# Window attention with turned keys and turned queries copied out of PSUM by two engines

## The chip, the cores and the metric

The kernel runs on one core of a Trainium2 chip. The metric is the device time of one execution in microseconds (us), lower is better. A core has TensorE (PE in the rows: matmuls and transposes; PEld is its weight load), VectorE (DVE), ScalarE (ACT), GpSimd (POOL) and the sync engine SyncE (SP), which here only issues DMAs. Each engine takes its instructions in the order in which the program gives them; the engines are tied together by semaphores written out by hand.

## What is computed

A Swin-style block on a (4, 32, 32, 128) image, then a single-head self-attention over the 1024 tokens of each image. What matters here is the first attention:

```python
xn = _layer_norm(x, norm1_g, norm1_b)               # 64 windows of 64 tokens after a roll
qkv = xw @ qkv_w.T + qkv_b                           # 16 heads of 8 channels
q = _rope2d(q, tabs); k = _rope2d(k, tabs)
attn = einsum('bhnd,bhmd->bhnm', q * scale, k) + attn_mask
attn = softmax(attn, axis=-1)
out = einsum('bhnm,bhmd->bhnd', attn, v)             # then projection, residual
# then layer norm, a gated MLP (fc1, silu, fc2), and x + y
# second block: f = x Wq, g = x Wk, h = x Wv; gamma * softmax(f g^T) h + x
```

## The kernel before, in words

The 64 windows are taken two at a time: 32 pairs of 128 tokens. Values of fp32 are split into an fp16 high part and an fp16 low part, so that TensorE can work in fp16. A software pipeline of steps n = -2 to 34 runs over the pairs; the same `body(n, ...)` is written once for each engine, and the order of its parts is the order in which the engine works. Steps 12 to 27 are a hardware loop of 8 steps, the others are written out.

In step n TensorE (`pe_pairs`, lines 908 to 968) does: the projection of queries and keys of pair n+2 (L917), the turn (transpose) of queries and keys of pair n+1 into the bank `T1_BANK` (L932, L933; the helper's line is L904), the scores of pair n with the mask (L938; helper lines L876, L885), whose row maxima VectorE takes (L1075), the scores in the turned direction of pair n-1 (L949; L876, L897), probabilities times values of pair n-3 (L956), the value projection of pair n-1 (L964), and the turn of the queries with their maxima for pair n (L968). `t1_ps` is one PSUM bank of 2 KB per partition seen as fp16: half 0 holds the turned queries, half 1 the turned keys, 512 elements each.

In step n VectorE multiplies by the rotary tables for pair n+2 (L1048, `ta`, `tb`), copies both halves of `t1_ps` for pair n+1 to `qk_t` (L1060) and signals `qt_ready`, subtracts for `v_lo` (L1068), takes the maxima (L1075), splits them (L1080, L1082), and so on. SyncE waits for `qt_ready` and then issues four DMAs (L836) that put the turned keys from `qk_t` into `k_t`; they signal `kz_ready`, for which the scores of the next step wait (L936).

In step n ScalarE (L1149 to L1209) writes `q_rows` and `k_rows` (L1158, L1161; all copies have the helper's line L1117) from the rotated values `rot` that GpSimd has made (L1253), then in some steps `ln_hi_of` (below), the exponential (L1187, `e_buf`), the copy of the turned queries with maxima (`q_t`), two halves of `v_hi`, and `p_hi`.

The layer norm of the input goes in 8 chunks of 512 tokens. Chunks 2 to 7 are turned by TensorE in steps n = 1, 3, 5, 7, 9 and 11 (`LN_STEP`), in the bank `T1_BANK` too, between the scores of pair n and the turned scores of pair n-1:

```python
if ln_chunk(n):
    pe.wait_ge(qt_ready, n + 2)      # T1_BANK has been copied out for pair n+1
    ln_turn(ln_chunk(n))             # L845
```

ScalarE then copies the turned chunk (`xn_all`, `ln_hi_of`), VectorE subtracts (`ln_lo_of`, L1011). For chunks 4 to 7 ScalarE also normalises two tiles of `xn` at the end of each of the steps 3 to 10 (L1208). In steps 28 and later the MLP's first work is mixed in. The time after 205 us (MLP and second attention) is not touched.

Of the kernel before, what the change touches and what calls it, by code (L numbers as in the profile page):

```python
# [26 lines left out]
PAIRS = WPAIRS * B  # L27
# [25 lines left out]
def build(nc, t):  # L53
    ctx = ExitStack()
    with ctx:
# [3 lines left out]
        def sem(name):  # L59
            return ctx.enter_context(nc.semaphore(name))  # L60
# [120 lines left out]
        lo_done = sem("lo_done")  # L181
        t1_done = sem("t1_done")
        qt_ready = sem("qt_ready")
        kz_ready = [sem(f"kz_ready{u}") for u in range(2)]
        s_done = sem("s_done")
        max_done = sem("max_done")
# [12 lines left out]
        def wait(eng, s, value):  # L199

            if not isinstance(value, int) or value > 0:
                eng.wait_ge(s, value)
# [135 lines left out]
        def mlp_pe(pe):  # L338
# [37 lines left out]
            def turn_a_waits(c):  # L376
                pe.wait_ge(a_lo, c + 1)
                wait(pe, at_ready, c)
                if at_bank(c) == PRJ_BANK:
                    pe.wait_ge(x1_ready, c)  # L380
# [83 lines left out]
            def early(left):  # L464
                if left == 5:

                    pe.wait_ge(rope_done, PAIRS)
                    turn_a_waits(0)
                    turn_a(0, 0)
                if left == 4:  # L470

                    pe.wait_ge(qt_ready, PAIRS)
                    pe.wait_ge(proj_w_lo, 1)
                    project(0, 0)
                if left == 3:

                    bias()
                if left == 2:

                    pe.wait_ge(fc1_b_ready, 1)  # L480
                    turn_a_waits(1)
                    turn_a(1, 1)
                    pe.wait_ge(mlo_done, PAIRS)
                    turn_y(0, 0)
                if left == 1:

                    pe.wait_ge(exp_done, PAIRS)
                    pe.wait_ge(fc1_w_lo, 1)
                    fc1(0, 0, 0)

            def bias():

                pe.wait_ge(rest_loaded, REST_LOADS)
                pe.wait_ge(at_ready, 1)
                for k in range(2 * HBLK):
                    last = pe.matmul(ps[:, at_bank(0), k:k + 1], fc1_w[:, 128 * k:128 * k + 128], g1b1[:, 3:4],
                                     start=True, stop=True)
                last.then_inc(fc1_b_sum, 1)

            return body, early, bias  # L500

        def mlp_dve(dve):
# [240 lines left out]
        with ExitStack() as st:  # L743
# [15 lines left out]
            qk_t = tmp("qk_t", [128, 2, 2, 4, 128], F16)  # L759
# [11 lines left out]
            t1_ps = ps[:, T1_BANK, :].bitcast(F16).rearrange("p (a c q) -> p a c q", a=2, c=4)  # L771
# [34 lines left out]
            def at_step(n, step):  # L806
                return isinstance(n, int) and n == step

            def valid(n, lag):
                return not isinstance(n, int) or 0 <= n - lag < PAIRS  # L810
# [29 lines left out]
            def pe_pairs(pe):  # L840
# [38 lines left out]
                def scores(queries, keys, w, parts):  # L879

                    masked(S_BANK, w, 0, parts)
                    for c in range(4):
                        for e in range(2):
                            rows = slice(64 * e, 64 * e + 64)
                            last = pe.matmul(  # L885
                                ps[rows, S_BANK + c // 2, 256 * (c % 2):256 * (c % 2) + 256]
                                .rearrange("p (h k) -> p h k", h=4),
                                queries[:, c, rows], keys[:, :, c, rows], start=False, stop=True, skip_group_check=True)
                    return last
# [18 lines left out]
                def body(n, it, w, parts):  # L908
                    r = w % BUFS
                    u = r % 2  # L910
                    v = 1 - u

                    if valid(n, -2):
                        wait(pe, rope_done, n + 2)

                        pe.wait_ge(ln_ready, (n + 2) // TPC + 1 if isinstance(n, int) and n < LOOP_FROM else CHUNKS)
                        project(qkv_ps[:, 0:2 * DIM], n + 2, slice(0, 2 * DIM)).then_inc(qk_done, 1)  # L917
                    if at_step(n, -2):

                        pe.wait_ge(mask_top, 1)  # L920
                        pe.matmul(ps[0:1, T1_BANK, 0:1], mask_max[:], ln_const[:, 2, 0:1], start=True,
                                  stop=True).then_inc(mask_summed, 1)
                    if at_step(n, -1):

                        pe.wait_ge(mask_known, 1)
                        rest.append(pe.value_load(mask_any[0:1, 0:1].bitcast(mybir.dt.int32)))
                    if valid(n, -1):
                        wait(pe, lo_done, n + 2)
                        wait(pe, qt_ready, n + 1)
                        if ln_chunk(n, 1):  # L930
                            pe.wait_ge(ln_ready, ln_chunk(n, 1) + 1)
                        turn(t1_ps[:, 0], q_rows[:, (r + 1) % BUFS])  # L932
                        turn(t1_ps[:, 1], k_rows[:, v]).then_inc(t1_done, 1)  # L933
                    if valid(n, 0):

                        pe.wait_ge(kz_ready[u], it * 64 + 64)  # L936
                        wait(pe, mlo_done, n)
                        scores(qk_t[:, u, 0], k_t[:, r], w, parts).then_inc(s_done, 1)  # L938
                    if ln_chunk(n):

                        pe.wait_ge(qt_ready, n + 2)
                        ln_turn(ln_chunk(n))
                    if valid(n, 1):

                        wait(pe, q2_ready, n)
                        wait(pe, exp_done, n - 1)
                        if at_step(n, 1):
                            pe.wait_ge(ln_ready, 2)
                        scores_turned(k_t[:, (r - 1) % BUFS], q_t2[:, v], (w - 1) % WPAIRS, parts).then_inc(st_done, 1)  # L949
                    if valid(n, 3):  # L950
                        wait(pe, plo_done, n - 2)
                        wait(pe, norm_done, n - 3)
                        for hp in range(HP):
                            out = pv_ps[:, hp].rearrange("p e r d -> p (e r d)")
                            for k, (p, vals) in enumerate(((p_hi, v_hi), (p_hi, v_lo), (p_lo, v_hi))):
                                last = pe.matmul(out, p[:, v, 2 * hp:2 * hp + 2, :].rearrange("p h q -> p (h q)"),  # L956
                                                 vals[:, v, hp].rearrange("p e r d -> p (e r d)"),
                                                 start=(k == 0 and hp == 0), stop=(k == 2), skip_group_check=True)
                        last.then_inc(pv_done, 1)
                    if valid(n, 1):  # L960

                        wait(pe, vlo_done, n - 1)
                        wait(pe, q2_ready, n)
                        project(v_ps, n - 1, slice(2 * DIM, 3 * DIM)).then_inc(v_done, 1)  # L964
                    if valid(n, 0):
                        wait(pe, mlo_done, n + 1)
                        wait(pe, q2_ready, n)
                        turn(t2_ps, q_rows[:, r]).then_inc(t2_done, 1)  # L968
                    if at_step(n, -2):
                        ln_turn(1)  # L970
# [11 lines left out]
            def _(dve):  # L982
# [55 lines left out]
                def body(n, it, w):  # L1038
                    r = w % BUFS
                    u = r % 2  # L1040
                    v = 1 - u
# [15 lines left out]
                    if valid(n, -1):  # L1057

                        dve.wait_ge(t1_done, n + 2)
                        dve.tensor_copy(qk_t[:, v], t1_ps).then_inc(qt_ready, 1)  # L1060
                    if at_step(n, -1):
                        ln_stats_of(3)
                    if valid(n, 2):
# [42 lines left out]
            def _(act):  # L1106
# [9 lines left out]
                def copy(out, in_):  # L1116
                    return act.activation(out, in_, ACT.Copy)  # L1117
# [31 lines left out]
                def body(n, it, w):  # L1149
                    r = w % BUFS  # L1150
                    u = r % 2
                    v = 1 - u
                    if isinstance(n, int):
                        mlp_act(act)[2](LAST - n)
                    if valid(n, -2):

                        act.wait_ge(r_done, n + 3)
                        copy(q_rows[:, (r + 2) % BUFS, :, 0:16].rearrange("p h (r d) -> p h r d", r=2),  # L1158
                             rot[:, u, 0].unsqueeze(2).broadcast_to([128, HEADS, 2, HD]))
                        wait(act, t1_done, n + 1)  # L1160
                        copy(k_rows[:, u].rearrange("p h (r d) -> p h r d", d=HD)[:, :, 0:3:2, :],  # L1161
                             rot[:, u, 1].unsqueeze(2).broadcast_to([128, HEADS, 2, HD])).then_inc(hi_done, 1)
                    if at_step(n, -2):
                        ln_hi_of(1)
                    if at_step(n, -1):
# [682 lines left out]
```

## Time and profile before

| | us |
|---|---|
| median of 3 runs | 410.07 |
| lowest, highest run | 408.0, 411.35 |
| the profiled execution's time | 408.14 |
| its span (first to last instruction) | 406.3 |
| steps 3 to 12 (window of 38 to 88 us): TensorE busy | 45.70 of 50.00 |
| same window: ScalarE, VectorE busy | 43.34, 42.23 |
| steps 13 to 29 (88 to 175 us): TensorE busy | 83.98 of 87.00 |
| same window: ScalarE, VectorE busy | 68.74, 74.96 |

The profile is of one execution; 1.8 us of its time lie outside the span. Busy times count an instruction from its start to its end, also where it overlaps the next one on its engine, so a share near 90% can be an engine without a gap. The chain of waits follows the last instruction back to what released it.

### The profile page before, as it was taken

Reading aid. Unit: us, or ns where it says so; the run is one execution under the profiler, and the core shown is the slowest. Engines: PE = TensorE matmul, PEld = TensorE weight load, DVE = VectorE, ACT = ScalarE, POOL = GpSimd, SP = SyncE. Lnnn points to the kernel's source line nnn. Section 1 sums busy time; section 2 is a strip of 40 time slices with the busy share of each in tenths; the row PEclk is TensorE's granted clock in tenths of the full one; section 3 lists DMA queues with packets and bytes.
Section 4 is the critical chain, followed back from the end, with each engine's and each line's share of the span. In section 5 each row is a group of like instructions: output and inputs, shape, how many; then the busy total and the mean of one; then the engine's idle time right before and its main releaser. Section 6 shows DMA issues by size and latency. Waiting matters only on the chain.

```text
span 406.3 us, 12124 instructions
## 1 busy us (share of the span) xinstructions
PE 357.3 (88%) x4700; PEld 223.4 (55%) x4700; DVE 300.9 (74%) x830; ACT 272.5 (67%) x436; POOL 261.0 (64%) x314
## 2 busy tenths in 40 slices
PE   2487999899998999998599999999989989989692
PEld 0244665555565666667355345553546757667472
DVE  6668888888888888887746767778657797884524
ACT  3467988887777787887635554444767867768480
POOL 7467967666767777797658665564235865868330
PEclk9999999999999999999989999999999999999787
DMA  5701110001101011110000100000101011010101
GB/s 173 250 15 27 29 27 26 25 24 30 31 27 29 25 29 29 29 29 3 0 3 2 26 2 0 2 2 0 28 0 28 2 52 27 2 54 2 53 2 55
DMA packets 15594, 12.19 MB, mean 30 GB/s; under 512 B 3991, under 2 KB 14136, under 8 KB 15544
## 3 DMA queue, kind: packets, MB, share of 16 engines
q1 hardware_dynamic: 14208, 10.96, 9.4%
q8 instruction: 34, 0.56, 0.6%
q10 hardware_dynamic: 1336, 0.54, 0.5%
q14 instruction: 16, 0.13, 0.1%
HBM read 4.15 MB, written 2.10 MB: 15 GB/s over the span
## 4 chain that ended last, share of the span: by engine, by line
PE 63%; DVE 15%; ACT 5%; DMA 5%; issue 5%; POOL 3%; SPq 2%; ACTq 1%; DVEq 0%; POOLq 0%
PE ps L347 8%; PE ps L1551 7%; PE ps L876 6%; PE ps L904 5%; PE ps L956 4%; PE ps L897 4%; DMA k_t<-qk_t 3%; PE ps L866 3%; PE ps L885 3%; PE ps L361 3%; SPq L836 2%; PE ps L868 2%; DVE ob L1687 2%; PE ps L1386 2%; DVE mx L1656 2%
## 5 line engine op out<-in xcount | busy, mean ns | idle before, releaser
L1738 POOL TENSOR_TENSOR el<-e,eh 128x1024 f16<-128x1024 f32 x28 | 59.7, 2131 | 42.0 <-ACT eh L1730 41.7
L1261 POOL TENSOR_TENSOR p_lo<-e_buf,p_hi 128x1024 f16<-128x1024 f32 x32 | 68.2, 2131 | 4.9 <-ACT p_hi L1117 2.9
L347 PE MATMUL ps<-y_t,fc_w 128*128 128x512 f16 x192 | 46.4, 383 | 4.0 <-POOL al L273 2.5
L1253 POOL TENSOR_TENSOR rot<-ta,tb 128x256 f32<-128x256 f32 x32 | 23.3, 728 | 38.9 <-DVE tb L1048 38.1
L1723 ACT ACTIVATE e<-ps 128x1024 f32<-128x1024 f32 x32 | 32.7, 1022 | 21.1 <-PE ps L1540 19.5
L1551 PE MATMUL ps<-val,eh 128*128 128x129 f16 x512 | 38.3, 225 | 7.5 <-DVE ob L1687 7.0
L876 PE MATMUL ps<-mask,identb 128*128 128x512 bf16 x128 | 39.4, 391 | 5.4 <-DMA k_t<-qk_t 5.2
L1075 DVE TENSOR_REDUCE ps<-ps 128x16 f32<-128x1024 f32 x32 | 39.4, 1233 | 6.0 <-PE ps L885 5.2
L1187 ACT ACTIVATE e_buf<-ps 128x1024 f32<-128x1024 f32 x32 | 32.7, 1023 | 14.5 <-PE ps L897 11.4
L1551 PEld LDWEIGHTS ps<-val,eh 128*128 128x128 f16 x512 | 32.8, 100 | 16.4 <-issue 9.9
L288 POOL TENSOR_TENSOR hl<-hid,hh 128x512 f16<-128x512 f32 x24 | 27.6, 1157 | 21.5 <-DVE yn L537 11.5
L1656 DVE TENSOR_REDUCE mx<-ps 128x1 f32<-128x1024 f32 x24 | 29.3, 1222 | 11.0 <-PE ps L1524 10.8
L1117 ACT ACTIVATE p_hi<-e_buf 128x1024 f16<-128x1024 f32 x32 | 33.8, 1057 | 0.8
L1730 ACT ACTIVATE eh<-e 128x1024 f16<-128x1024 f32 x32 | 33.7, 1054 | 0.7
L646 ACT ACTIVATE sg<-ps,fc_bias 128x512 f32<-128x512 f32 x32 | 21.9, 685 | 17.9 <-PE ps L347 17.6
L508 DVE SCALAR_TENSOR_TENSOR hid<-ps,fc_bias,sg 128x512 f32<-128x512 f32 x32 | 23.9, 746 | 11.2 <-PE ps L347 8.9
L866 PE MATMUL ps<-qkv_w,xn_all 128*128 128x128 f16 (+1 forms) x192 | 27.7, 255 | 5.0 <-ACT mask L1117 3.4
L904 PE MATMUL ps<-ident,q_rows 128*128 128x128 f16 x256 | 26.3, 227 | 6.0 <-DVE q_rows L1082 3.7
L347 PEld LDWEIGHTS ps<-y_t,fc_w 128*128 128x128 f16 x192 | 17.3, 98 | 25.9 <-issue 4.7
L1117 ACT ACTIVATE q_t<-ps 128x512 f16<-128x512 f16 x32 | 19.1, 596 | 10.7 <-PE ps L904 10.4
L897 PEld LDWEIGHTS ps<-q_t,k_t 128*64 128x64 f16 x1024 | 18.7, 113 | 13.6 <-issue 13.6
L1551 PE MATMUL ps<-val,el 128*128 128x129 f16 x256 | 23.8, 226 | 0.0
(166 smaller groups left out, 959.8 us busy)
## 6 DMA issues: line engine op xcount, KB each, us to landing
k_t<-qk_t SPq DMA_DIRECT2D x126, 32.0 KB, 1.9
x_all<-in_x SPq DMA_DIRECT2D x8, 256.0 KB, 4.9
out<-ob SPq DMA_DIRECT2D x8, 192.0 KB, 2.1
yr<-xr SPq DMA_DIRECT2D x16, 64.0 KB, 2.0
mask_f<-in_mask SPq DMA_DIRECT2D x1, 512.0 KB, 3.7
fc_w<-in_fc_w SPq DMA_DIRECT2D x1, 512.0 KB, 6.2
out<-ob SPq DMA_DIRECT2D x4, 128.0 KB, 2.4
fc_w<-in_fc_w SPq DMA_DIRECT2D x1, 256.0 KB, 6.1
```

What stands on the lines that cost most here:

```text
L347: last = pe.matmul(ps[:, bank, :], fc1_w16[:, ws, 128 * block_:128 * block_ + 128], y_t[:, v, ys, :], start=(n == 0), stop=(n == 2))
L866: pe.matmul(out, xn_all[:, at(i, 1), xs, :].rearrange("p a q -> p (a q)"), qkv_w16[:, ws, cols], start=(n == 0), stop=False, skip_group_ch ...
L876: pe.matmul(ps[:, bank + b, :].rearrange("p (h k) -> p h k", h=8), identb[:], mm, start=(part == 0), stop=False, skip_group_check=True)
L897: last = pe.matmul(ps[rows, ST_BANK + h // 8, WTOK * (h % 8):WTOK * (h % 8) + WTOK], keys[:, h % 4, h // 4, rows], queries[:, h // 4, rows ...
L904: last = pe.transpose(out[:, c, :], rows[:, 4 * c:4 * c + 4, :].rearrange("p h r -> p (h r)"), ident16[:])
L1075: dve.tensor_reduce(mx_ps, ps[:, S_BANK:S_BANK + 2, :].rearrange("p b (h k) -> p (b h) k", h=8), AX.X, ALU.max).then_inc(max_done, 1)
L1117: return act.activation(out, in_, ACT.Copy)
L1261: pool.tensor_tensor(p_lo[:, u], e_buf[:, u], p_hi[:, u], ALU.subtract).then_inc(plo_done, 1)
L1551: return pe.matmul(pv4[:, j, i, 0:DIM + 1], weights[:, T % H_BUFS, 128 * n:128 * n + 128], val[:, b % 2, part, m, 0:DIM + 1], start=first, ...
L1656: dve.tensor_reduce(mx[:, k:k + 1], two(S4), AX.X, ALU.max, negate=True).then_inc(max4_done, 1)
L1730: act.activation(eh[:, T % H_BUFS, :], e4[:, T % E_BUFS, :], ACT.Copy).then_inc(eh_done, 1)
L1738: pool.tensor_tensor(el[:, T % H_BUFS, :], e4[:, T % E_BUFS, :], eh[:, T % H_BUFS, :], ALU.subtract).then_inc(el_done, 1)
```

## The change

VectorE now copies only the half with the turned keys and signals `qt_ready`. ScalarE waits for `qt_ready`, copies the half with the turned queries in the same step, behind `k_rows`, and signals a new semaphore `qq_ready`. SyncE's DMAs still wait for `qt_ready`. Wherever TensorE waited for `qt_ready` it now waits for `qq_ready`, and the scores (L938) wait for it too. The wait for `qt_ready` keeps the two copies, which read the same bank, one behind the other.

```diff
@@ PE
-                    pe.wait_ge(qt_ready, PAIRS)
+                    pe.wait_ge(qq_ready, PAIRS)
...
-                        wait(pe, qt_ready, n + 1)
+                        wait(pe, qq_ready, n + 1)
...
                         pe.wait_ge(kz_ready[u], it * 64 + 64)
                         wait(pe, mlo_done, n)
+                        pe.wait_ge(qq_ready, n + 1)
                         scores(qk_t[:, u, 0], k_t[:, r], w, parts).then_inc(s_done, 1)
                     if ln_chunk(n):
 
-                        pe.wait_ge(qt_ready, n + 2)
+                        pe.wait_ge(qq_ready, n + 2)
                         ln_turn(ln_chunk(n))
@@ DVE
                         dve.wait_ge(t1_done, n + 2)
-                        dve.tensor_copy(qk_t[:, v], t1_ps).then_inc(qt_ready, 1)
+                        dve.tensor_copy(qk_t[:, v, 1], t1_ps[:, 1]).then_inc(qt_ready, 1)
@@ ACT
                         copy(k_rows[:, u].rearrange("p h (r d) -> p h r d", d=HD)[:, :, 0:3:2, :],
                              rot[:, u, 1].unsqueeze(2).broadcast_to([128, HEADS, 2, HD])).then_inc(hi_done, 1)
+                    if valid(n, -1):
+
+                        act.wait_ge(qt_ready, n + 2)
+                        copy(qk_t[:, v, 0], t1_ps[:, 0]).then_inc(qq_ready, 1)
                     if at_step(n, -2):
                         ln_hi_of(1)
```

On ScalarE, at the border of steps 6 and 7, these rows stood before (`xn` is the normalised input, `xn_all` the copy of the turned chunk, `e_buf` the exponential):

```order
L1131 ACTIVATE xn<-x_all,nmr,rstd 128x128
L1117 ACTIVATE q_rows<-rot 128x16x16 [waits r_done]
L1117 ACTIVATE k_rows<-rot 128x32x8 [waits t1_done]
L1117 ACTIVATE xn_all<-ps 128x4x128 [waits ln_turned]
L1187 ACTIVATE e_buf<-ps 128x1024 [waits plo_done,st_done]
```

and with the change these stand there:

```order
L1133 ACTIVATE xn<-x_all,nmr,rstd 128x128
L1119 ACTIVATE q_rows<-rot 128x16x16 [waits r_done]
L1119 ACTIVATE k_rows<-rot 128x32x8 [waits t1_done]
L1119 ACTIVATE qk_t<-ps 128x512 [waits qt_ready]
L1119 ACTIVATE xn_all<-ps 128x4x128 [waits ln_turned]
L1193 ACTIVATE e_buf<-ps 128x1024 [waits plo_done,st_done]
```

The new row stands behind `xn`, `q_rows` and `k_rows` of the same engine and ahead of all else of the step; every step from -1 to 30 has one. On TensorE no row moves, but the one that turns a chunk waits for another engine. In step 1 these rows stood before:

```order
L876 MATMUL ps<-mask,identb 128x512 [waits mlo_done,kz_ready1]
L876 MATMUL ps<-mask,identb 128x512
L885 MATMUL ps<-k_t,qk_t 64x256 x8
L845 MATMUL ps<-ident,xn 128x128 [waits ln_norm,qt_ready]
L845 MATMUL ps<-ident,xn 128x128 x3
L876 MATMUL ps<-mask,identb 128x512 [waits ln_ready,q2_ready]
```

and with the change:

```order
L877 MATMUL ps<-mask,identb 128x512 [waits qq_ready,mlo_done,kz_ready1]
L877 MATMUL ps<-mask,identb 128x512
L886 MATMUL ps<-k_t,qk_t 64x256 x8
L846 MATMUL ps<-ident,xn 128x128 [waits ln_norm,qq_ready]
L846 MATMUL ps<-ident,xn 128x128 x3
L877 MATMUL ps<-mask,identb 128x512 [waits ln_ready,q2_ready]
```

The chunk's turn now needs ScalarE's copy of the same step; the scores need that of the step before.

## Rows read from the trace of the kernel before

**Rows 1.** The page's first line: span and instructions.
```profile
span 406.3 us, 12124 instructions
```

**Rows 2.** Busy time by stretch: window, PE, PEld, DVE, ACT, POOL busy (x instructions), clock, DMA.
```profile
38.00:88.00 50.00, 45.70 (x820) 29.92 (x820) 42.23 (x106) 43.34 (x86) 37.23 (x57) 1.00 0.11 28
88.00:175.00 87.00, 83.98 (x1548) 52.79 (x1549) 74.96 (x193) 68.74 (x126) 65.28 (x88) 1.00 0.10 27
```

**Rows 3.** Chain of waits, steps 3 to 11: start us, us, what.
```profile
41.00 0.59 PE ps L845 x4
...
51.82 0.61 PE ps L845 x4
...
60.68 1.06 ACT p_hi L1117
61.73 0.78 ACT xn L1131 x2
...
62.65 0.63 PE ps L845 x4
...
73.85 0.59 PE ps L845 x4
...
84.66 0.63 PE ps L845 x4
```

**Rows 4.** Timeline of ScalarE, steps 6 and 7: start us, us, instruction.
```profile
58.03 0.40 ACT L1117 ACTIVATE k_rows<-rot 128x256 f16<-128x256 f32 x1
58.46 1.02 ACT L1187 ACTIVATE e_buf<-ps 128x1024 f32<-128x1024 f32 x1
59.57 0.60 ACT L1117 ACTIVATE q_t<-ps 128x512 f16<-128x512 f16 x1
60.06 0.59 ACT L1117 ACTIVATE v_hi<-ps 64x128 f16<-64x128 f32 x2
...
62.41 0.40 ACT L1117 ACTIVATE q_rows<-rot 128x256 f16<-128x256 f32 x1
62.72 0.40 ACT L1117 ACTIVATE k_rows<-rot 128x256 f16<-128x256 f32 x1
```

**Rows 5.** Timeline of VectorE in step 26: the copy and what follows.
```profile
163.65 0.68 DVE L1060 COPY qk_t<-ps 128x1024 f16<-128x1024 f16 x1
164.25 0.59 DVE L1068 TENSOR_TENSOR v_lo<-ps,v_hi 64x128 f16<-64x128 f32 x2
```

**Rows 6.** Chain of waits in step -1.
```profile
17.20 0.59 DVE qk_t L1060
...
17.81 0.62 ACTq L1170
```

**Rows 7.** Timeline of ScalarE in step 1.
```profile
30.09 0.40 ACT L1117 ACTIVATE k_rows<-rot 128x256 f16<-128x256 f32 x1
30.73 0.60 ACT L1117 ACTIVATE xn_all<-ps 128x512 f16<-128x512 f32 x1 [0.24 <-PE ps L845]
31.80 1.02 ACT L1187 ACTIVATE e_buf<-ps 128x1024 f32<-128x1024 f32 x1 [0.46 <-PE ps L897]
32.72 0.59 ACT L1117 ACTIVATE q_t<-ps 128x512 f16<-128x512 f16 x1
```

**Rows 8.** Timelines of VectorE in step 1 and of ScalarE in step 3.
```profile
31.78 0.68 DVE L1011 TENSOR_TENSOR xn_all<-ps,xn_all 128x512 f16<-128x512 f32 x1
...
41.56 0.42 ACT L1117 ACTIVATE q_rows<-rot 128x256 f16<-128x256 f32 x1 [0.56 <-POOL rot L1253]
```

**Rows 9.** What TensorE waited for, 20 to 180 us, then 75 to 180: us, times, longest.
```profile
PE ps L876 <- DMA k_t<-qk_t: 5.1, 6, 1.1
...
PE ps L876 <- DMA k_t<-qk_t: 2.7, 3, 0.9
```

**Rows 10.** Timeline of ScalarE in step 27, in brackets its idle time before.
```profile
165.73 1.02 ACT L1187 ACTIVATE e_buf<-ps 128x1024 f32<-128x1024 f32 x1 [0.43 <-PE ps L897]
167.12 0.60 ACT L1117 ACTIVATE q_t<-ps 128x512 f16<-128x512 f16 x1 [0.36 <-PE ps L904]
```

More of the change, by code:

```diff
@@ L183, in build @@
         qt_ready = sem("qt_ready")
+        qq_ready = sem("qq_ready")
         kz_ready = [sem(f"kz_ready{u}") for u in range(2)]
```

## The prediction, made before the changed kernel ran

> **What bounds the kernel now.** I read the busy time by stretch first. From 38 to 88 us, which is about steps 3 to 12, TensorE is busy 45.70 of 50.00 and ScalarE 43.34, VectorE 42.23; from 88 to 175 us TensorE is busy 83.98 of 87.00 and ScalarE only 68.74 [rows 2]. So there are two regimes. In the later one the bound is TensorE, and ScalarE has about a fifth of its time free. In the earlier one ScalarE is nearly as full as TensorE, for it also normalises two tiles per step and copies a turned chunk every second step. The chain of waits says the same with an order in it: TensorE's turns of the chunks (L845) start at 41.00, 51.82, 62.65, 73.85 and 84.66 us, so 10.82, 10.83, 11.20 and 10.81 apart, and the chain reaches the one of 62.65 through ScalarE's `p_hi` and `xn`, which ends at 62.51 [rows 3]. Two steps there take 5.4 us each although later steps take 4.8: the stretch is a loop through ScalarE. ScalarE's timeline of step 6 shows no gap: `k_rows` at 58.03 and for 0.40, the exponential at 58.46, `q_t` at 59.57, `v_hi` at 60.06 [rows 4].
>
> Where ScalarE is the bound, work moved to it lengthens the kernel. And the turn of a chunk now waits for a ScalarE copy that stands behind `xn`, `q_rows` and `k_rows` of the same step, where it waited for a VectorE copy that was long done.
>
> **The parts that can gain.** VectorE's copy of 1024 elements takes 0.68 and the next instruction starts 0.60 after it [rows 5]. Half the elements are not in the trace of before on this engine. From below the saving is nothing, from above half of the 0.60, 0.30. I take 0.27, because 0.15 or so of such an instruction looks fixed: the difference between 0.68 and 2 x 0.27 for the elements. The keys' DMAs start earlier by as much. TensorE waited for them six times and 5.1 us in all from 20 to 180 us, but only three times and 2.7 us after 75 us [rows 9]. Each of the later three shrinks by 0.27: -0.8 us. The three early ones lie in the stretch that ScalarE bounds, so nothing is booked for them. All other steps are paced by TensorE's own work, and there an earlier VectorE gives nothing.
>
> The Trainium skill ("VectorE: DVE Perf Modes", the section on the TRN2 errata) gives a copy out of PSUM as a fixed 120 cycles plus elements over the speed-up on VectorE at 0.96 GHz, and 172 cycles plus elements on ScalarE at 1.2 GHz. By an estimate from that table the whole copy is 0.66 us, which agrees with the 0.68 of [rows 5], the half 0.39, and ScalarE's half 0.57: 0.96 us of engine time in place of 0.66, so the fixed part is paid twice and the rule speaks against splitting. With its 0.57 in place of the row's 0.60 the sum below would be about 0.2 us lower.
>
> **ScalarE's new copy.** It has a twin: `q_t`, 512 fp16 elements out of PSUM, 0.60 us, and the next copy starts 0.49 after it (60.06 - 59.57). An instruction that reads PSUM behind `k_rows` starts 0.43 after it (58.46 - 58.03) [rows 4]. So in a step without slack the copy costs ScalarE 0.49, and a waiting engine sees it done at `k_rows` + 0.43 + 0.60. From ScalarE's end to TensorE's turn another 0.14 pass (62.51 to 62.65) [rows 3].
>
> *Step -1.* ScalarE's copy goes ahead of its two DMA issues and the mask's copy, which are on the chain: VectorE's copy 17.20, DMA issue 17.81 [rows 6]. If an issue does not wait for the copy ahead of it, the chain is 0.27 shorter; if it waits, 0.60 - 0.27 = 0.33 longer. I take 0.
>
> *Step 1.* `k_rows` starts at 30.09, so the new copy ends at 30.09 + 0.43 + 0.60 = 31.12 and the turn can start at 31.26. Before, `xn_all` followed the turn at 30.73; less 0.63 for the turn and 0.05 to hand over, the turn started at 30.05. It is 1.2 late. `xn_all` then ends at 30.73 + 1.2 + 0.60 = 32.53, where VectorE's subtraction from the same chunk started at 31.78 [rows 7, 8]: VectorE is 0.8 late, and in steps 1 and 2 the chain goes through VectorE's statistics and on to GpSimd's `rot`, for which ScalarE's `q_rows` of step 3 waits (idle 0.56 before 41.56) [rows 8].
>
> *Step 3.* From the start of `q_rows` to the turn: 0.31 to `k_rows` (62.72 - 62.41), 0.43, 0.60, 0.14, together 1.48 [rows 3, 4]. 41.56 + 0.8 + 1.48 = 43.84 in place of 41.00: **+2.84**.
>
> *Steps 5, 7, 9, 11.* Follow ScalarE from one turn to the next. In the even step between, the exponential moves 0.49 later. `q_t` behind it had some slack: elsewhere it starts 0.92 after the exponential's start (32.72 - 31.80) [rows 7], here 59.57 - 58.46 = 1.11, because TensorE's turn was last; so 0.19 is absorbed and `q_t`, `v_hi`, `p_hi`, `xn`, `q_rows` are 0.30 late. In the odd step the turn starts 1.48 after `q_rows` in place of 0.24 (62.65 - 62.41), 1.24 more [rows 3, 4]. Together 1.54 in two steps: the distance of turns becomes 10.83 + 1.54 = 12.37. Against 10.82, 10.83, 11.20, 10.81 that is 1.55 + 1.54 + 1.17 + 1.56 = **+5.8**; the 11.20 held a DMA wait that is now covered.
>
> *Behind step 11.* Per step ScalarE idles 0.43 before the exponential and 0.36 before `q_t` [rows 10]; the copy fits in at 0.49, pushing the exponential by some 0.1, which the second gap takes. No cost from steps 12 to 30. If that cover were gone, all of the copy's excess would be paid 16 to 18 times. The scores' new wait is for a copy of the step before, over two us old by then. In the last steps the chain is TensorE's and VectorE's again; nothing is booked.
>
> **Sum.** 2.84 + 5.8 - 0.8 = 7.8. The profiled execution took 408.14 us with a span of 406.3 [rows 1], so its successor takes 416.0. The median of the three runs is 1.9 higher, which gives 417.9. I predict 417.0, between the two.
>
> **Rivals.**
>
> *Only the added work of ScalarE counts.* TensorE needs less than 5.4 us for a step in the early stretch (4.8 later), so it may catch up what a late turn costs. Then steps 3 to 11 pay 0.49 each, 9 x 0.49 = 4.4, less 0.8: +3.6, 411.7 from the profiled time, 413.6 from the median. Against it: behind the turn the chain goes on through TensorE's turned scores and the queries' turn into ScalarE, so the lateness comes back to ScalarE itself. Chance 0.16.
>
> *ScalarE becomes the bound of the loop too.* Its gaps of 0.79 per step [rows 10] must take the copy of 0.49 to 0.60; if the wait for `qt_ready`, the start behind `k_rows` or jitter makes it 0.2 more than fits, 16 steps pay 3.2: 419.2 from the profiled time, 421.1 from the median. For it: GpSimd's `rot` comes only just before `q_rows`, so the 0.79 can't be moved about. It decides once the copy costs over 0.8. Chance 0.12.
>
> *Faster.* If ScalarE reached the new copy before TensorE finished the scores in the six steps with a chunk, the turns would lose nothing, and an earlier start of the keys' DMAs could clear all 5.1 us of waits [rows 9]: 403.0 from the profiled time, 405.0 from the median. It needs `k_rows` at least 1.2 us earlier against the turn than in [rows 3, 4, 7], and nothing moves it. Chance 0.03.
>
> *My forecast* as worked out, 413.8 to 420: 0.69.
>
> **Numbers.** A measurement of this kernel tells about 1% from no change, 4.1 us here, so "the same" ends at 414.2. The first rival lies mostly below it (0.14), my forecast's lower edge adds 0.03: same 0.17, faster 0.03, slower 0.80. For the range: the unknown costs are -0.3 to +0.3 in step -1, 0 to 0.3 for each of three DMA waits, and the 1.9 between profiled time and median; with half of the first rival and most of the second, 412.8 to 421.0.
>
> **What would show it.** VectorE's half copy near 0.41 us and ScalarE's near 0.60. TensorE's turns of chunks 3 to 7 12.4 us apart, the last of them near 93 us in place of 84.66, and before each an idle stretch of TensorE of about 1.2 us or more that ends with ScalarE's `qk_t`. Busy ScalarE in that stretch without gaps except for the turn. Steps 13 to 29 as long as before, with the exponential later by about 0.1. I am wrong if the turns stay 10.8 apart, which would mean that ScalarE had slack that I didn't see; or if the steps behind 12 lengthen, which is the second rival; or if the half copy on VectorE does not get shorter, which would take away the 0.8.

## The result and the profile after

The change made the kernel slower: 419.92 us in the median of 4 runs (416.9 to 421.78), against 409.04 in that set for the kernel before (408.0 to 411.35). The ratio is 1.0265 with a 95% interval of 1.0213 to 1.0317, about 10.8 us. The profiled execution took 419.65 us. Forecast were 417.0 us and a range of 412.8 to 421.0.

The page of the changed kernel, its first two rows, answers to [rows 1]:

```profile
span 417.8 us, 12159 instructions
...
PE 361.5 (87%) x4700; PEld 226.7 (54%) x4700; DVE 297.1 (71%) x830; ACT 288.6 (69%) x468; POOL 260.9 (62%) x314
```

VectorE's busy time fell by 3.8 us in all (300.9 before, 297.1 now), ScalarE's rose by 16.1. What TensorE waited for, over the whole span (us, times, longest), answers to [rows 9]:

```profile
PE ps L846 <- ACT qk_t L1119: 11.3, 6, 2.3
...
PE ps L877 <- DMA k_t<-qk_t: 3.9, 6, 0.8
```

The first row is new, and it is the result in one line: six waits, one for each turn of a chunk, all for ScalarE's copy of the queries, 11.3 us together. The waits for the keys' DMAs shrank from 5.2 us in seven waits to 3.9 in six. The turns of the chunks in steps 3, 5, 7 and 9 in TensorE's timeline (start us, us, in brackets the idle time before and what ended it) answer to [rows 3]:

```profile
43.97 0.68 PE L846 MATMUL ps<-ident,xn 128*128 128x128 f32 x4 [2.11 <-ACT qk_t L1119]
...
57.44 0.66 PE L846 MATMUL ps<-ident,xn 128*128 128x128 f32 x4 [1.50 <-ACT qk_t L1119]
...
69.74 0.66 PE L846 MATMUL ps<-ident,xn 128*128 128x128 f32 x4 [2.31 <-ACT qk_t L1119]
...
82.04 1.12 PE L846 MATMUL ps<-ident,xn 128*128 128x128 f32 x4 [1.33 <-ACT qk_t L1119]
```

and that of step 11 with what TensorE does around it:

```profile
92.72 0.63 PE L886 MATMUL ps<-k_t,qk_t 128*64 128x256 f16 x8
95.67 1.12 PE L846 MATMUL ps<-ident,xn 128*128 128x128 f32 x4 [2.31 <-ACT qk_t L1119]
96.57 1.06 PE L877 MATMUL ps<-mask,identb 128*128 128x512 bf16 x2
```

The scores end at 93.35 and TensorE idles until 95.67. The distances are 13.47, 12.30, 12.30 and 13.63 us in place of about 10.9 (TensorE's timeline of before has the turns of steps 3 to 11 at 40.94, 51.80, 62.65, 73.78 and 84.66). Two things are in them. The 12.30 is the loop through ScalarE. The 13.5 come with a turn, or the work behind it, that runs at half speed: the turn of step 11 takes 1.12 us where that of step 7 takes 0.66. TensorE's granted clock around step 11 (window, busy us and matmuls, clock, DMA):

```profile
93.00:95.60 2.60, 0.35 (x8) 1.00 0.14 38
95.60:98.70 3.10, 3.03 (x43) 0.51 0.07 16
98.70:101.00 2.30, 2.30 (x44) 0.91 0.00 0
```

Here the clock is at 2.4 GHz (1.00) while TensorE idles and at 1.2 GHz for about 3 us when it works again. In steps 3 to 11 of this profile that happened at the waits of steps 3, 9 and 11 and not at those of steps 5 and 7. Before, from 38 to 175 us, it was never low (clock 1.00 in [rows 2]). In step 1 the clock was low already when the wait began. These rows of step 1 show it, for the turns take 0.40 us as at the high clock and the mask's two matmuls right behind them 0.98 where they take 0.59 at the high clock:

```profile
26.88 0.40 PE L905 MATMUL ps<-ident,q_rows 128*128 128x128 f16 x4
27.11 0.39 PE L905 MATMUL ps<-ident,k_rows 128*128 128x128 f16 x4
27.33 0.98 PE L877 MATMUL ps<-mask,identb 128*128 128x512 bf16 x2
```

It fell at 27.4 us and rose again at 34.2. In the kernel before, and in a second profile of the changed one, the same two matmuls of step 1 take 1.06 us although the clock column reads 1.00 there: for the first 30 us and more the column alone can't be trusted, the durations can.

ScalarE's timeline of steps 6 and 7 answers to [rows 4]:

```profile
64.13 0.60 ACT L1119 ACTIVATE qk_t<-ps 128x512 f16<-128x512 f16 x1
64.62 1.02 ACT L1193 ACTIVATE e_buf<-ps 128x1024 f32<-128x1024 f32 x1
65.53 0.60 ACT L1119 ACTIVATE q_t<-ps 128x512 f16<-128x512 f16 x1
...
67.59 0.86 ACT L1133 ACTIVATE xn<-x_all,nmr,rstd 128x128 f32<-128x128 f32 x2
68.36 0.40 ACT L1119 ACTIVATE q_rows<-rot 128x256 f16<-128x256 f32 x1
68.67 0.40 ACT L1119 ACTIVATE k_rows<-rot 128x256 f16<-128x256 f32 x1
69.09 0.60 ACT L1119 ACTIVATE qk_t<-ps 128x512 f16<-128x512 f16 x1
70.43 0.60 ACT L1119 ACTIVATE xn_all<-ps 128x512 f16<-128x512 f32 x1 [0.75 <-PE ps L846]
```

The new copy takes 0.60 us and the exponential starts 0.49 after it. Between two turns ScalarE idles only for the turn (0.75 us in the last row) and then, behind it, 0.46 before the exponential and 0.34 before `q_t` (step 5). The copy of step 7 ends at 69.69 and the turn starts at 69.74. Behind step 12 the copy fits in, as these rows of step 13 show, which answer to [rows 10]:

```profile
107.18 0.40 ACT L1119 ACTIVATE k_rows<-rot 128x256 f16<-128x256 f32 x1
107.60 0.60 ACT L1119 ACTIVATE qk_t<-ps 128x512 f16<-128x512 f16 x1
109.26 1.02 ACT L1193 ACTIVATE e_buf<-ps 128x1024 f32<-128x1024 f32 x1 [1.06 <-PE ps L898]
```

and VectorE's half copy is short, as against [rows 5]:

```profile
170.22 0.42 DVE L1062 COPY qk_t<-ps 128x512 f16<-128x512 f16 x1
170.56 0.59 DVE L1070 TENSOR_TENSOR v_lo<-ps,v_hi 64x128 f16<-64x128 f32 x2
```

Where the 11.5 us between the two spans lie, by the start of the same work in both traces: the turn of step 3 is 3.03 late (43.97 against 40.94), that of step 11 is 11.01 late (95.67 against 84.66), the scores of pair 12 are 12.37 late, those of pair 30 are 11.06 late, and the end is 11.5 late. So all of it comes from the steps up to 12; the loop gives 1.3 back, the rest adds 0.4.

### The profile page after: what moved, and what is told of

Same layout as the page of the kernel before. It is cut to its first block, busy times and chain, and to the rows that moved or that the text cites. A ratio compares the mean times of both kernels' runs of the same rounds, so it can differ in the third digit from the quotient of the medians.

```text
span 417.8 us, 12159 instructions
## 1 busy us (share of the span) xinstructions
PE 361.5 (87%) x4700; PEld 226.7 (54%) x4700; DVE 297.1 (71%) x830; ACT 288.6 (69%) x468; POOL 260.9 (62%) x314
## 4 chain that ended last, share of the span: by engine, by line
PE 52%; ACT 14%; DVE 14%; issue 8%; POOL 7%; DMA 2%; SPq 1%; ACTq 0%; DVEq 0%; POOLq 0%
PE ps L348 8%; PE ps L1557 7%; ACT p_hi L1119 4%; PE ps L877 4%; PE ps L362 3%; PE ps L958 3%; PE ps L905 3%; PE ps L898 3%; DVE ob L1693 2%; ACT v_hi L1119 2%; PE ps L1392 2%; PE ps L1540 2%; DVE mx L1662 2%; PE ps L886 2%; DMA k_t<-qk_t 2%
## 5 line engine op out<-in xcount | busy, mean ns | idle before, releaser
L877 PE MATMUL ps<-mask,identb 128*128 128x512 bf16 x128 | 41.1, 405 | 3.9 <-DMA k_t<-qk_t 3.9
L1662 DVE TENSOR_REDUCE mx<-ps 128x1 f32<-128x1024 f32 x24 | 29.3, 1222 | 12.3 <-PE ps L1530 12.1
L509 DVE SCALAR_TENSOR_TENSOR hid<-ps,fc_bias,sg 128x512 f32<-128x512 f32 x32 | 23.9, 746 | 10.9 <-PE ps L348 8.6
L898 PEld LDWEIGHTS ps<-q_t,k_t 128*64 128x64 f16 x1024 | 20.1, 118 | 15.2 <-issue 15.2
```

The source lines that it names most:

```text
L877: pe.matmul(ps[:, bank + b, :].rearrange("p (h k) -> p h k", h=8), identb[:], mm, start=(part == 0), stop=False, skip_group_check=True)
L1662: dve.tensor_reduce(mx[:, k:k + 1], two(S4), AX.X, ALU.max, negate=True).then_inc(max4_done, 1)
```

## Experiments

Ratios are to the kernel before on the same chip. Theory A is the one behind the prediction: the chunk's turn waits for a copy behind ScalarE's other work, and the loop through ScalarE is longer by that and by the copy. Theory B is the first rival: only ScalarE's added work counts.

### VectorE copies both halves, keys first

```diff
 dve.tensor_copy(qk_t[:, v, 1], t1_ps[:, 1]).then_inc(qt_ready, 1)
+dve.tensor_copy(qk_t[:, v, 0], t1_ps[:, 0]).then_inc(qq_ready, 1)
-act.wait_ge(qt_ready, n + 2)
-copy(qk_t[:, v, 0], t1_ps[:, 0]).then_inc(qq_ready, 1)
```

> VectorE copies both halves itself, keys first (signals qt_ready), then queries (signals qq_ready); ScalarE copies neither. All waits of the changed kernel stay. Theory A (the loss is the wait of the chunks' turns for a copy that stands behind ScalarE's other work): the turns are back to 10.8 us apart, TensorE's waits for qt/qq copies vanish, and what is left is the earlier signal to the keys' DMAs, -0.8 to -1.3 us, less up to 0.5 for the second copy's fixed part in steps 1 and 2, where VectorE is on the chain: ratio 0.997 to 1.000 to the kernel before. Theory B (the loss is ScalarE's added work alone) expects the same here, since ScalarE's work is as before. If splitting itself costs (more semaphores, longer total copy), 1.005 or more.

Measured: 408.34 us, ratio 1.0007 (0.9976 to 1.0039). The turns are 10.90 to 11.21 apart. All of the loss is gone, though each semaphore of the changed kernel and each wait of TensorE for it is still there. The two half copies on VectorE:

```profile
163.37 0.41 DVE L1062 COPY qk_t<-ps 128x512 f16<-128x512 f16 x1
163.70 0.42 DVE L1063 COPY qk_t<-ps 128x512 f16<-128x512 f16 x1
164.03 0.59 DVE L1071 TENSOR_TENSOR v_lo<-ps,v_hi 64x128 f16<-64x128 f32 x2
```

They start 0.33 apart and together hold VectorE 0.66 us in place of 0.60, so splitting alone costs 0.06 per step and gives the DMAs 0.27. No gain of that shows in the time: the expected 0.8 to 1.3 us are smaller than the interval.

### VectorE copies both halves in the six chunk steps only

```diff
 dve.tensor_copy(qk_t[:, v, 1], t1_ps[:, 1]).then_inc(qt_ready, 1)
+if ln_chunk(n):
+    dve.tensor_copy(qk_t[:, v, 0], t1_ps[:, 0]).then_inc(qq_ready, 1)
-if valid(n, -1):
+if valid(n, -1) and not ln_chunk(n):
     act.wait_ge(qt_ready, n + 2)
```

> The changed kernel, but in steps 1, 3, 5, 7, 9 and 11 VectorE copies both halves (keys, then queries), so that no turn of a chunk waits for ScalarE; in all other steps ScalarE copies the queries. Theory A: the six waits of 11.3 us go, TensorE's clock stays high there, left are 0.30 us for each of the five even steps 2 to 10 (+1.5) and -1.0 from the DMA waits: ratio 1.000 to 1.003. Theory B (added work of ScalarE, 0.49 per step it copies in, also on top of the clock's share): five of ten early steps still carry it, about half of the loss stays: 1.010 to 1.014.

Measured: 407.52 us, ratio 0.9971 (0.9941 to 1.0001). Theory B's 1.010 to 1.014 is out: with 26 of the 32 ScalarE copies still in place the loss is gone. That is a little below the 1.000 to 1.003 expected. The last four turns are 11.13 apart, 0.26 over the 10.87 that is usual before, where 0.30 were expected. TensorE's waits for a ScalarE copy of the queries are gone; what it waits for before the turns is again `xn`:

```profile
PE ps L846 <- ACT xn L1135: 3.2, 4, 1.2
```

One thing in this profile was not expected. The granted clock fell at 39.5 us, in the middle of matmuls without a gap and before the turn of step 3, which waited for nothing; these rows are at half speed:

```profile
39.52 1.06 PE L877 MATMUL ps<-mask,identb 128*128 128x512 bf16 x2
40.51 1.06 PE L886 MATMUL ps<-k_t,qk_t 128*64 128x256 f16 x8
```

TensorE's last idle time of over 1 us had ended at 37.96 (1.29 us, for VectorE). So the clock can fall in the early steps without a wait for ScalarE's copy.

> The version in which VectorE copies both halves in the six chunk steps and ScalarE the queries in all others, once more for its time: its first ratio was 0.9971 (0.9941 to 1.0001). Theory A: the loop behind step 12 gains 0.5 to 1.6 us and the even steps give back 0.3 each; 0.996 to 1.000 again. If the gain is real the two intervals together lie below 1.

Measured: 407.31 us, ratio 0.9983 (0.9960 to 1.0006). Each interval reaches 1. Taken together, by an estimate from the scatter of all runs, they give 0.998 with an interval that ends just below 1 (0.9996). So a gain of 0.2% is at the edge of what these runs can tell. The clock fell before the turn of step 3 in this profile too, at 39.2 us.

### ScalarE's work alone

```diff
+if valid(n, -1):                       # ScalarE, at the new copy's place
+    copy(spare[:], ident16[:].unsqueeze(1).broadcast_to([128, 4, 128]))
```

> The kernel before, with one extra ScalarE copy of 512 fp16 elements (from a constant in SBUF to a spare buffer) at the place of the new copy in every step; nobody waits for it. It is the added ScalarE work by itself. Theory A: the even steps pass on 0.30 each (4 to 5 of them, +1.2 to 1.5), in the odd ones it lies in the 0.2 and 0.46 that ScalarE waits for TensorE: ratio 1.002 to 1.005. Theory B: it explains the loss, 9 to 10 steps of 0.5 and more: 1.011 to 1.026.

Measured: 409.25 us, ratio 1.0023 (0.9990 to 1.0056). The last turns are 11.18 apart, 0.31 more than before, which is the 0.30 of the prediction. The rows of steps 6 and 7:

```profile
63.54 0.40 ACT L1118 ACTIVATE k_rows<-rot 128x256 f16<-128x256 f32 x1
63.84 0.61 ACT L1118 ACTIVATE spare<-ident 128x512 f16<-128x512 f16 x1
64.47 0.60 ACT L1118 ACTIVATE xn_all<-ps 128x512 f16<-128x512 f32 x1
65.20 1.02 ACT L1190 ACTIVATE e_buf<-ps 128x1024 f32<-128x1024 f32 x1
```

In the odd step the extra copy lies where ScalarE would have waited for the turn and the scores. Theory B falls a second time: the work by itself costs about 1 us, and the interval doesn't exclude 0.

### The wait alone

```diff
 pe.wait_ge(qt_ready, n + 2)
+pe.wait_ge(hi_done, n + 3)             # ScalarE's k_rows of the same step
 ln_turn(ln_chunk(n))
```

> The kernel before with one more wait and no work added: in the six chunk steps TensorE's turn waits for ScalarE's k_rows copy of the same step (hi_done), the instruction ahead of which the new copy stands behind. Theory A: the turn starts k_rows' end + 0.14 = 0.31 + 0.40 + 0.14 = 0.85 after q_rows in place of 0.24, so the turns are 10.87 + 0.61 = 11.5 us apart, the one of step 3 at 41.56 + 0.15 + 0.85 = 42.6 in place of 40.94: in all +1.6 + 4 x 0.6 = 4.0 us, ratio 1.009 to 1.011. Theory B (no work added to ScalarE, so no loss): 1.000.

Measured: 412.15 us, ratio 1.0102 (1.0066 to 1.0138), 4.2 us where 4.0 were worked out, and turns 11.40 to 11.42 apart from step 3 on; the turn of step 3 is 1.9 late, where 1.6 were worked out. The clock was low around step 1 here too (27.1 to 33.9 us) and at 1.00 behind it up to the end of step 11, so the distances are free of it and that 1.9 may not be. ScalarE's `k_rows` and TensorE's turn in step 7:

```profile
65.17 0.40 ACT L1118 ACTIVATE k_rows<-rot 128x256 f16<-128x256 f32 x1
```

```profile
65.67 0.63 PE L845 MATMUL ps<-ident,xn 128*128 128x128 f32 x4 [1.45 <-ACT k_rows L1118]
```

One wait, with not an instruction added that works, costs more than the added work does. Wait (0.54 over the 10.87 of before), work (0.31) and the copy's own end behind `k_rows` (69.69 less 69.07, 0.62) add up to 1.47; the changed kernel's turns at the high clock are 1.43 further apart than before.

### The copy ahead of `q_rows` in the chunk steps

```diff
+if ln_chunk(n):                        # ahead of q_rows and k_rows
+    act.wait_ge(qt_ready, n + 2)
+    copy(qk_t[:, v, 0], t1_ps[:, 0]).then_inc(qq_ready, 1)
 ...
-if valid(n, -1):                       # behind them
+if valid(n, -1) and not ln_chunk(n):
```

> The changed kernel, but in the six chunk steps ScalarE copies the queries ahead of q_rows and k_rows in place of behind them; its work is the same. Theory A (the chunk's turn waits for what stands ahead of the copy on ScalarE): the turn starts 0.31 + 0.43 = 0.74 us earlier against q_rows, so the turns are 12.30 - 0.74 = 11.56 us apart where the clock stays high, and the first term shrinks by 0.74 and what VectorE passes on: 3.7 to 5 us less than the changed kernel, ratio to the kernel before 1.014 to 1.018. Theory B (ScalarE's added work alone) expects no difference to the changed kernel, 1.026.

Measured: 411.57 us, ratio 1.0066 (1.0034 to 1.0099). The last turns are 11.69 apart, 0.61 less than 12.30 (0.74 expected). The difference is in these rows: behind `xn` the copy starts after 0.89, where `q_rows` starts after 0.77.

```profile
51.39 0.86 ACT L1133 ACTIVATE xn<-x_all,nmr,rstd 128x128 f32<-128x128 f32 x2
52.28 0.60 ACT L1119 ACTIVATE qk_t<-ps 128x512 f16<-128x512 f16 x1
52.77 0.41 ACT L1119 ACTIVATE q_rows<-rot 128x256 f16<-128x256 f32 x1
```

TensorE's waits for the copy fell from 11.3 to 6.6 us. But the time fell by 8 us, more than the 3.7 to 5 expected. In this profile the clock stayed at 2.4 GHz in all steps from 3 to 12, though two of the waits were still 1.71 us long, and the scores of pair 12 start 9.0 us earlier than in the changed kernel (92.52 against 101.53). So the work at half clock went with the shorter waits; that the shorter waits are the cause is likely and not shown by one profile.

### The split only from step 12 on

```diff
 dve.tensor_copy(qk_t[:, v, 1], t1_ps[:, 1]).then_inc(qt_ready, 1)
+if isinstance(n, int) and n < LOOP_FROM:
+    dve.tensor_copy(qk_t[:, v, 0], t1_ps[:, 0]).then_inc(qq_ready, 1)
```

(and ScalarE's copy is left out in the same steps)

> ScalarE copies the queries only from step 12 on, VectorE both halves (keys first) in the steps before. Theory A: no loss in the early stretch, and from step 12 on the gain of the earlier signal to the DMAs (-0.8 to -1.3): turns 10.9 apart, ratio 0.996 to 1.000, like the version in which only the chunk steps were VectorE's (0.997). If the loop after step 12 carries a cost of ScalarE's copy that the other runs hide, over 1.003.

Measured: 407.55 us, ratio 0.9984 (0.9954 to 1.0013). The loop carries no hidden cost of ScalarE's copy: the second rival (ScalarE becomes the loop's bound) is out. From the scores of pair 12 to those of pair 30 it takes 87.7 us; the changed kernel 87.9, the kernel before 89.2, VectorE doing both halves 88.6, but the kernel before with the idle ScalarE copy 88.5. Two profiles of one version differ by up to 1.0 here (88.7 and 87.7 for the version with six steps on VectorE, 89.2 and 88.1 for the one of the next section), so differences of that size carry no weight.

### TensorE kept at work before the turn

```diff
+wait(pe, exp_done, n - 1)              # the bank is free; in step 1 also ln_ready
+for _ in range(5):
+    pe.matmul(ps[:, ST_BANK, :]..., identb[:], mask16..., start=True, stop=True)
 pe.wait_ge(qq_ready, n + 2)
 ln_turn(ln_chunk(n))
```

> The changed kernel with five extra matmuls of 512 columns (0.27 us each, results overwritten) on TensorE right before it waits for the queries' copy in the six chunk steps, so that TensorE works for 1.35 us of the 1.1 to 2.3 us that it waits. Turns start when ScalarE's copy is done either way. Theory A with a clock part (the granted clock fell to half for some 4 us after the waits of steps 1, 3, 9 and 11, at 1.2 us each): some or all of these go, -2.4 to -4.8 us against the changed kernel, ratio to the kernel before 1.015 to 1.021. If the lower clock is not what made the turns 13.5 in place of 12.3 us apart, the ratio stays at 1.026.

Measured: 418.91 us, ratio 1.0250 (1.0212 to 1.0288), where 1.015 to 1.021 were expected. In the profile the cure works where it is applied. Step 11 there, with the five extra matmuls:

```profile
90.61 1.25 PE L947 MATMUL ps<-mask,identb 128*128 128x512 bf16 x5
93.00 0.66 PE L846 MATMUL ps<-ident,xn 128*128 128x128 f32 x4 [1.13 <-ACT qk_t L1126]
```

The turn takes 0.66 us again, the turns are 12.45 and then four times 12.30 us apart, and the scores of pair 12 start at 97.53 in place of 101.53. From step 3 to 11 the clock fell at seven of the ten waits in the two profiles of the changed kernel (the second stands below), and at none here. So TensorE's idling before the turn goes with the lower clock around it, and the lower clock makes 12.3 into 13.5. But the profiled execution takes 0.6 us longer than that of the changed kernel. From the scores of pair 30 to the end it is 231.8 us in place of 228.4, and the clock shows one reason; first the changed kernel in the stretch behind pair 30, then this one:

```profile
187.00:215.00 28.00, 22.32 (x415) 1.00 0.04 10
```

```profile
187.00:198.60 11.60, 10.58 (x230) 0.99 0.05 13
198.60:209.00 10.40, 8.16 (x118) 0.52 0.02 3
209.00:215.00 6.00, 2.95 (x15) 1.00 0.00 0
```

Behind 215 us both have some 3 us more at half clock.

> The changed kernel with five extra matmuls before each chunk's turn once more. In its first profile the turns were 12.30 us apart throughout and the scores of pair 12 began 4.0 us earlier than in the changed kernel, but from the scores of pair 30 to the end 231.8 us passed in place of 228.4, with the granted clock at half for 10 us where the changed kernel has 3.4. If this giving back belongs to the kernel, a second profile has it too (230 us or more behind pair 30) and the ratio is again 1.023 to 1.027. If it was chance, the second profile shows 227 to 229 us there and the ratio 1.016 to 1.021.

Measured: 418.62 us, ratio 1.0250 (1.0208 to 1.0292). The second profile has turns 12.24 to 12.31 apart from step 3 on, 230.6 us behind pair 30, and again ten microseconds at half clock:

```profile
197.00:207.60 10.60, 8.51 (x154) 0.52 0.01 2
```

So the giving back was there in both profiles, and the times agree with it: 418.91 and 418.62 us are 1.0 less than the changed kernel's 419.92 and 419.60, and not the 4 of the early stretch. But this part of the kernel scatters by itself. Every version that ran has some stretch at half clock between 187 and 220 us, where the attention gives way to the MLP, and one and the same version, the one with six steps on VectorE, had 10 us of it and took 229.9 us behind pair 30 in its first profile, and 3 us and 226.7 in its second. With the extra matmuls it is the longest, some 14 us in all both times, against 3 and 7 in the changed kernel. Why is not settled.

### The changed kernel again

> The changed kernel once more, for a second profile: whether the granted clock falls in the same steps (1, 3, 9 and 11) and whether the turns' distances of 13.5 and 12.3 us come at the same places. If the clock's falls differ from execution to execution, the distances move with them while those at the high clock stay at 12.30; the ratio stays at 1.022 to 1.031.

Measured: 419.60 us, ratio 1.0266 (1.0215 to 1.0317). The turns are 13.18, 13.14, 12.30, 13.56 and 13.58 apart: the clock fell in part at other turns than in the first profile (steps 3, 7, 9 and 11), and the one distance at the high clock is 12.30 again. At step 7 it fell while TensorE still waited, as these windows around the turn at 69.80 show:

```profile
69.30:69.80 0.50, 0.00 (x1) 0.01 (x1) 0.00 (x0) 0.44 (x1) 0.50 (x1) 0.60 0.24 66
69.80:72.80 3.00, 3.00 (x42) 2.04 (x43) 0.69 (x1) 0.60 (x1) 0.97 (x4) 0.50 0.06 16
```

Behind the scores of pair 30, 228.4 us pass in the first profile and 228.5 in this one.

## Why the prediction was right, and where it was short

*What bounds the kernel.* The two regimes were there. All the loss lies before step 12, and the ones that moved a wait (the wait alone, the copy ahead) moved the turns' distance as the loop through ScalarE says.

*The keys' DMAs.* Booked -0.8 us. From the scores of pair 12 to those of pair 30 it took 1.3 us less. That is of the size, but two profiles of one version differ by up to 1.0 there, and one version with the earlier signal took as long as the kernel before (89.2 us). So not even the sign is shown. The half copy takes 0.42 us, 0.41 were expected.

*ScalarE's copy.* 0.60 us and 0.49 to the next instruction: as its twin, `q_t`. The start behind `k_rows`, 0.43, was 0.42. The hand-over to TensorE was booked at 0.14 and is 0.05 in step 7. The table of the Trainium skill ("VectorE: DVE Perf Modes", the section on the TRN2 errata), by which the estimates were 0.39 for VectorE's half and 0.57 for ScalarE's, is 0.03 low for both. By durations its rule that the fixed part is paid twice is borne out: the two half copies on VectorE take 0.41 and 0.42 against 0.68 for the whole, 0.15 more, and the table gives 0.13. What VectorE loses is less, for the copies overlap: from the start of the first to the next instruction 0.66 us pass in place of 0.60.

*Steps 1 and 3.* Booked +2.84, measured 3.0 in the first profile and 3.4 in the second (the turn of step 3 at 43.97 and 44.36 against 40.94; the prediction's 41.00 is the chain's time for it). Inside, the turn of step 1 was 0.96 late (31.00 against 30.04) where 1.2 were booked, and from `q_rows` of step 3 to the turn 1.40 passed where 1.48 were booked. TensorE worked at half clock behind the turn of step 1, which was not booked.

*Steps 5 to 11.* Booked 12.37 per two steps, measured 12.30 where the clock is high; in all +5.8 booked, +8.0 measured. The step that was short is here. The sum treated a waiting TensorE as costing the wait and nothing else. Around three of the five waits it worked at 1.2 GHz for some 3 us, which made two of the four distances 1.2 and 1.3 longer, and 1.4 more were lost between the turn of step 11 and the scores of pair 12. That is 3.9 us of the first profile, about the whole gap between the 11.5 found and the 7.8 predicted. The term was left out though [rows 2] showed the clock as 1.00 over a stretch in which TensorE never idled over 1.1 us at a time, which says nothing on longer gaps. The forecast of 417.0 came closer to the 419.92 measured than the sum's 416.0 by luck: it had 1.0 us added for runs slower than the profiled one, and that gap turned out to be 0.3.

How much of it is the clock's in the *time*, and not only in that stretch, stays open. With TensorE kept at work the early stretch is 4 us shorter and the time no more than 1 us. With the shorter waits of the version that copies ahead of `q_rows` the time fell by 8 us, of which the waits (11.3 less 6.6 us) are 4.7.

*Step -1* was booked at 0, and that holds. From TensorE's projection at 11.20 us to the one at 20.22 that waits for the mask, 9.02 us pass before; with the change it is 9.08 and 9.06 in the two profiles. That the scores of pair 1 started 1.1 us earlier than before in the first profile and 0.1 later in the second comes from the clock: around 26 us four turns take 0.40 in the first, and 0.61 in the second and before.

*The rivals.* Only ScalarE's work: 1.0023, out. ScalarE as the bound of the loop: out by the version that splits only there. Faster: out, for the time rose.

## What to carry to other kernels

Before moving an operation to an engine with free time on average, look at what stands ahead of it in that engine's order at its new place, and at who waits for it: here the wait alone, with no work added, cost 4 us and the work alone 1, while the whole change cost 11. Read the free time in the stretch where the operation runs, since ScalarE's 21% of free time behind step 12 were no help to the steps in which it was full. Where a move makes TensorE wait, look at the granted clock of the work behind the wait too; filling the waits with extra matmuls repaired the place and not the time.

## What the runs showed of the hardware

TensorE's granted clock fell around a wait, and not at a fixed place in it. In the first profile of the changed kernel work resumed at 43.97, 82.04 and 95.67 us, and the clock fell to 1.2 GHz at 44.48, 82.03 and 95.68, each time for some 3 us. In the second, work resumed at 69.80, 83.36 and 96.94 and the clock had fallen at 69.40, 83.06 and 96.71, while TensorE idled; at step 3 it fell 1.15 us after the turn's start (45.51 against 44.36). It did so at some waits only: the idle stretch of 2.31 us before the turn of step 7 left no trace in the first profile, the one of 2.31 us before step 11 did, and in the second it was steps 3, 7, 9 and 11. Nor did it need the wait: in both profiles of the version with six steps on VectorE it fell at 39.5 and 39.2 us, while TensorE worked, and with the wait alone it fell at none of the waits from step 3 to 11, up to 1.46 us long. With 1.25 us of extra matmuls in the same stretches it fell at none from step 5 on, in two profiles. Both of these have ten microseconds at half clock in one piece some 100 us later.

The Trainium skill ("PSUM — Partial Sum Buffer", the section on engine and sequencer instructions) has ScalarE's queue as strictly first in, first out, and every row of ScalarE shown here stands in the program's order. The runs show what that costs a wait: with the same copy moved ahead of two instructions of 0.40 us, TensorE's turns were 0.61 us closer together.

A ScalarE copy out of PSUM started 0.42 us behind `k_rows` (68.67 to 69.09), a copy out of SBUF at the same place 0.30 (63.54 to 63.84), neither waiting for another engine. It is no fixed rule: in step 1 the copy out of PSUM started 0.31 behind it.
